# GpSimd makes one of the eight inflow quads of each unit in a fused Mamba and mixture-of-experts kernel

## What is computed

```
deltaA   = exp(einsum('bdl,dn->bdln', delta, A))
deltaB_u = einsum('bdl,bnl,bdl->bdln', delta, B, uc)
state    = deltaA[t] * state + deltaB_u[t]
y[t]     = einsum('bdn,bn->bd', state, C[t])
```

## Time and profile before

| | us |
|---|---|
| median of 3 runs | 899.54 (898.86 to 904.14) |
| the profiled execution, its own time | 906.28 |
| its span in the trace | 904.5 |
| unit 0: from its first inflow to that of unit 1 | 80.8 |
| units 1, 2, 3, 4, 5 | 75.3, 74.3, 74.3, 74.4, 73.2 |
| units 6, 7 | 70.9, 62.6 |
| from there to the end (the last bookkeeping, the experts, the last layer norm) | 250.4 |

### The profile page before, as it was taken

One profiled execution on the slowest core, in us unless ns is written; L12 is line 12 of the kernel. 1 busy time (PEld: TensorE's weight loads), 2 busy tenths in 40 slices (PEclk: granted clock), 3 DMA queues, 4 the chain that ended last, 5 costly groups with the idle time before them and its releaser, 6 DMA issues. The chain is left out here.

```text
span 904.5 us, 11867 instructions
## 1 busy us (share of the span) xinstructions
PE 615.8 (68%) x2649; PEld 294.8 (33%) x2649; DVE 707.4 (78%) x1358; ACT 446.4 (49%) x904; POOL 583.6 (65%) x540
## 2 busy tenths in 40 slices
PE   3855768667685786865877766656540999889820
PEld 2221111222232131221222212212130888888820
DVE  2037888998998998999899899999932577777654
ACT  3545746655637646465464662523310555454425
POOL 5023566586698779779679959968864355554533
PEclk8675586786587576588769655556555899999975
DMA  3047546566467857646746655765102556566546
GB/s 81 0 101 174 134 93 155 136 151 140 104 163 157 229 127 162 150 110 157 166 120 152 141 135 137 162 146 133 38 27 80 161 174 179 163 174 173 170 135 176
DMA packets 67572, 123.64 MB, mean 137 GB/s; under 512 B 10240, under 2 KB 44864, under 8 KB 59312
## 3 DMA queue, kind: packets, MB, share of 16 engines
q1 hardware_dynamic: 63184, 113.90, 52.2%
q0 software_dynamic: 4320, 8.99, 3.2%
HBM read 100.21 MB, written 16.35 MB: 129 GB/s over the span
## 5 line engine op out<-in xcount | busy, mean ns | idle before, releaser
L509 POOL TENSOR_TENSOR hc<-hs,Crep 128x1024 f32<-128x1024 f32 x128 | 306.4, 2394 | 134.3 <-DVE hs L1246 107.8
L1246 DVE TENSOR_TENSOR_SCAN hs<-bank,state,flow 128x512 f32<-128x512 f32 x256 | 314.5, 1268 | 40.4 <-ACT bank L1017 34.4
L1017 ACT ACTIVATE bank<-bank,negA 128x512 f32<-128x512 f32 x256 | 166.8, 660 | 187.1 <-PE bank L724 186.6
L724 PE MATMUL bank<-dparts,sel 96*128 96x512 bf16 x256 | 130.5, 522 | 129.0 <-DVE hs L1246 120.5
L1236 DVE TENSOR_TENSOR flow<-flow,bank 128x2048 f32<-128x2048 f32 x64 | 145.1, 2267 | 13.0 <-issue 12.4
L724 PEld LDWEIGHTS bank<-dparts,sel 96*128 96x128 bf16 x256 | 27.9, 111 | 311.9 <-DVE hs L1246 256.7
L1168 ACT ACTIVATE flow<-bank,b1T 128x128 f32<-128x128 f32 x284 | 80.8, 368 | 81.1 <-PE bank L898 81.1
L733 PE MATMUL bank<-hc,kc 128*32 128x512 f32 x512 | 101.6, 878 | 17.6 <-DVE yg L1254 14.7
L898 PE MATMUL bank<-flow 128*128 128x128 f32 x568 | 83.3, 292 | 13.9 <-issue 6.9
L623 POOL DMA_INDIRECT results<-flow,idn x71 | 69.8, 982 | 33.4 <-issue 33.4
L682 PE MATMUL bank<-hT,wtapT 128*128 128x512 f32 x128 | 76.9, 741 | 15.9 <-ACT hT L953 11.6
(11 more groups left out here) (172 smaller groups left out, 885.1 us busy)
## 6 DMA issues: line engine op xcount, KB each, us to landing
flow<-du_d SPq DMA_DIRECT2D x64, 1024.0 KB, 7.2
flow<-L_ffn_W SPq DMA_DIRECT2D x71, 256.0 KB
dparts<-part SPq DMA_DIRECT2D x96, 64.0 KB, 3.1
xg<-xs SPq DMA_DIRECT2D x71, 66.0 KB
du_d<-du SPq DMA_DIRECT2D x32, 128.0 KB, 2.4
hs<-results SPq DMA_DIRECT2D x16, 256.0 KB, 4.4
xin<-L_attn_x SPq DMA_DIRECT2D x8, 256.0 KB, 3.3
out<-hc SPq DMA_DIRECT2D x8, 256.0 KB, 2.4
```

The lines of the kernel that those rows point to most:

```text
L509: nc.gpsimd.tensor_tensor(hc[:, Q % 2, two, :], hs[:, Q % 2, two, :], Crep[u % 2][:].unsqueeze(1).broadcast_to([P, 2, T]), ALU.mult).then_ ...
L724: nc.tensor.matmul(dbank[G % 3][:], sel[:, g // 4 % 4, :], dparts[u % 2][:, 4 * (g // 16) + g % 4, :])\
L1017: nc.scalar.activation(dbank[G % 3][:], dbank[G % 3][:], ACT.Exp, scale=negA[:, ch:ch + 1]).then_inc(s_ex, 1)
L1246: nc.vector.tensor_tensor_scan(hs[:, Q % 2, j, :], dbank[G % 3][:], flow[Q % 3][:, j, :], state[:, Q // QUADS % 2, Q % QUADS, j:j + 1], AL ...
```

## The change

POOL makes the inflow of quad 6 of each unit, as two products of 128x1024, behind its `times_c` of slots 9 and 10. It reads B from a copy in SBUF, `Bcopy`, which is the same memory as `xnT`. ACT makes the copy at the end of the unit before (`copy_b`). DVE leaves that `inflow` out; its scan at g = 24 waits for both products instead. The seven other inflows stay on DVE and go on reading B from PSUM. The rest are counts and waits that follow from it.

```diff
+        Bcopy = xnT
@@ SP
-                after(sp, s_bu, QUADS * (u - 1))
+                after(sp, s_bu, inflows_before(QUADS * (u - 1)))
+                after(sp, s_bp, 2 * (u - 1))
@@ POOL
+            def inflow_pair(u, pair):
+                Q = QUADS * u + POOL_QUAD
+                two = slice(2 * pair, 2 * pair + 2)
+                if pair == 0:
+                    pool.wait_ge(s_dul[Q % 3], 16 * (Q // 3 + 1))
+                    pool.wait_ge(s_bc, u + 1)
+                nc.gpsimd.tensor_tensor(flow[Q % 3][:, two, :], flow[Q % 3][:, two, :],
+                                        Bcopy[:].unsqueeze(1).broadcast_to([P, 2, T]), ALU.mult).then_inc(s_bp, 1)
@@ POOL host(j), right behind times_c
+                    if slot in (9, 10):
+                        inflow_pair(j, slot - 9)
@@ PE spread_b
-                after(pe, s_bu, QUADS * u)
+                after(pe, s_bu, inflows_before(QUADS * u))
+                after(pe, s_bc, u)
@@ ACT
+            def copy_b(u):
+                act.wait_ge(s_br, u + 1)
+                after(act, s_mf, 4 * (u - 2) + 3)
+                nc.scalar.copy(Bcopy[:], Brep[:]).then_inc(s_bc, 1)
@@ ACT xnT_evac
+                act.wait_ge(s_bp, 2 * min(u + 2, UNITS))
@@ ACT host(j)
+                    if g == 31 and late:
+                        copy_b(j + 1)
@@ DVE inflow
-                    dve.wait_ge(s_br, u + 1)
+                    dve.wait_ge(s_bc, u + 1)
@@ DVE scan
-                    dve.wait_ge(s_bu, Q + 1)
+                    if Q % QUADS == POOL_QUAD:
+                        dve.wait_ge(s_bp, 2 * (Q // QUADS) + 2)
+                    else:
+                        dve.wait_ge(s_bu, inflows_before(Q + 1))
@@ DVE host(j)
-                    if g % 4 == 0:
+                    if g % 4 == 0 and g // 4 != POOL_QUAD:
                         inflow(QUADS * j + g // 4)
```

More of the change, by code:

```diff
@@ L256, in mamba_moe @@
         s_bu = sem("inflow_done")
+        s_bc = sem("B_copied")
+        s_bp = sem("inflow_pairs_done_by_pool")
         s_sc = sem("scan_done")
@@ L309, in mamba_moe, with inflows_before @@
         s_out = [sem(f"out_stored{r}") for r in range(4)]
+        POOL_QUAD = 6
+        def inflows_before(Q):
+            return Q - (Q + QUADS - 1 - POOL_QUAD) // QUADS
         def tile_of(q, j):
@@ L1154, in _ @@
             act.wait_ge(s_negA, 1)
+            copy_b(0)
             for j in range(UNITS):
```

## The result

| | before | after |
|---|---|---|
| median | 899.71 us (4 runs, 898.86 to 904.14) | 921.88 us (4 runs, 921.16 to 922.67) |
| ratio, 95% interval | | 1.0228 (1.0197 to 1.026) |
| the profiled execution, its own time | 906.28 | 921.38 |
| its first scan starts at | 72.17 | 67.43 |

The change makes the kernel 22.2 us slower. The two profiled executions are only 15 us apart, because that of before began its scans 4.7 us late; from the first scan on they can be compared. Of the 22.2 us the scans hold 20.6 by these two traces; the rest is not placed. The table gives each unit from its first scan to the first scan of the next (unit 7 to the end of its last scan), which is 1 to 2 us off the spans by inflows shown ahead.

The account below looks back on a forecast made before the run. DVE was taken to set the scan phase's length, but POOL has no gap where its products go; unit terms 4.2 + 2.3 + 7.8 + 0.6 + 1.0 + 2.1 = 18.0 us on 899.5 gave 917.5 us, range 908.5 to 926.5.

Parts of the forecast that it names:

- The product's price: POOL's new product flow times Bcopy, priced like times_c: 2.31 us until the next instruction starts.
- The scan of g = 24: DVE's scan in unit 4 waits for both POOL products: 3.8 us later, not 2.35 earlier.
- The chain by `cnmr`: First product delays POOL's back_rstd, then ACT's xns, silus and decay, then DVE's scan of g = 25: +2.31 us.
- The unit's end: DVE's comparison L1288 lies blocked through POOL's indirect DMA and last product: unit end +2.6 us in units 2 to 4.
- rival 3: Indirect DMAs do not hold L1288 back at the end of units 2 to 4: 911.2 us, chance 0.2.
- Units 5 and 6: L1288 narrowly gets in behind slot 14's product: +0.6 and +1.0 us, otherwise +3.5 and +4.5.
- rival 1: L1288 is caught at the end of units 5 and 6 as well: 923.9 us, chance 0.24.
- Unit 1: No indirect DMAs, POOL has room at the end, L1288 meets the last product as before: +2.3 us.
- Rival 2: Products done before DVE reaches the scan of g = 24, each unit keeps 2.35 us: 880.7 us, chance 0.03.
- (a): Unit 0: POOL's products lie across delta_u and ahead of rest_delta, delaying mid_part and the scans: +4.2 us.
- (b): Units 1 to 5: POOL's first product stands ahead of cnmr, so the scan of g = 25 is late: +2.31 us.
- (c): Units 2 to 4: the block of one_hots at the unit's end moves with POOL; these units forecast at +2.6 us each.

Follow-up runs that it names:

- the first experiment: The changed kernel with back_rstd ahead of POOL's first product in slot 9 instead of behind it; 919.9 us, ratio 1.0212 (1.0169 to 1.0254).

## Why the prediction came out

The time, 921.88, lies 4.4 us above the forecast and inside its range. The units of the scans hold 2.6 us of that (20.6 against 18.0), most of it in unit 1; the rest is not placed by the two traces. By its own steps:

- **The product's price**: taken as 2.31, it is 2.30 (437.64 - 435.34). Right.
- **The scan of g = 24**: +3.8 forecast; from the unit's first scan it starts 55.72 us on in unit 4, before 51.95, so +3.77. The wait of 6 us is there in units 1 to 6.
- **The chain by `cnmr`**: +2.31 forecast; g = 25 is 58.47 us on after 56.15, +2.32. Right in size. But it was not the only bound there: the first experiment took it away and no gain is shown. Calling the bound by g = 24 and g = 27 "off the chain" did no harm to the sum (g = 27 is +2.41), but it would have misled anyone who repaired the order only.
- **The unit's end**: +0.3 us beyond the chain forecast (2.6 less 2.3), and 0.5 measured in units 2 to 4 (2.82 less 2.32). The size holds, but in part by luck, for the victim was another, which the prediction had not considered. The cast, an instruction ahead of the comparison, came up 0.61 us into the indirect DMA and was held for 2.82; the comparison behind it took 0.23. The mark of the prediction by which L1288 at 0.3 us supports rival 3 would have led astray: it should have been the time of the whole `one_hots`.
- **Units 5 and 6**: the narrow cases, +0.42 and +1.55 against 0.6 and 1.0. `one_hots` slipped in, so rival 1 fell. Timeline of unit 5 of after, DVE:

```profile
531.92 0.45 DVE L1318 CAST topf<-topi 128x8 f32<-128x8 uint32 x1
532.40 0.23 DVE L1321 TENSOR_TENSOR oh<-kc,topf 128x64 f32<-128x64 f32 x1
```

- **Unit 7**: 2.12 against 2.1. **Unit 0**: 3.95 against 4.2; `delta_u` took 2.82 beside the first product as forecast, and leaving that one unit's quad on DVE gave 3.8 back.
- **Unit 1**: 4.07 against 2.3, the one mis-sized term. "copy_b: nothing" looked only at the spot in a steady unit; in unit 0 the copy stands ahead of L992, and TensorE waits 0.92 us for it. Together with the lower granted clock at that place (0.61) it made a scan wait of 1.12. The other 0.65 us of the 1.77 are a smaller wait behind it (0.32) and parts that are not traced.
- **Load of quad 6, `low_delta`, SP's queue**: counted at nothing. DVE's waits for loads before inflows are 13.3 us in all after 13.0, and the new products had no idle time before them in any unit (the page's group of L527: 0.0).
- **Rival 2 and the sign**: the room of 134.3 us that POOL seemed to have the earlier trace rows has become 116.8, so 17.5 of the products' 37.5 us did find it, but not where it would have spared DVE the wait for them. With the room used at the right place, quad 1, the kernel is 1.1% faster instead of 2.3% slower.
- **Rival 3** said that indirect DMAs do not hold L1288 back, so that it is through before the last product. In time it is refuted (units 2 to 4 are 2.8 longer, not 0.5). What in such a DMA blocks is not settled, see below.

Of the three places, (a) is worth 3.8 us by the run with unit 0 on DVE. (b) is worth 13.2 where it is the only bound (the scan of g = 25 is 2.3 later in each of units 2 to 5, the rest lies in unit 1 and at the ends of units), and no gain is shown for it in after, where the bound by g = 24 is as high. (c), the moving of the block, adds 0.5 in each of units 2 to 4 and takes 1.9 and 2.5 away in units 5 and 6, where cast and comparison now take 0.45 + 0.23 and before took 0.17 + 2.47 and 0.14 + 3.01; that is why unit 5 is only 0.42 longer in spite of a chain that is 2.3 longer.

## What to carry to other kernels

Work moved to an engine with free time is worth only what that engine's free time is at the place where the result is wanted; read the timeline there, and everything that the moved instruction is put ahead of. Here two chains of equal height ended at one place, and repairing one of them showed no gain: before an order is repaired, work out what is late next, here to within 0.1 us. A cast of eight columns on VectorE cost 0.14 us here or two whole GpSimd products (4.89), by where it started, so put it where GpSimd has a gap.

## What the runs showed of the hardware beyond what was expected

A cast of eight columns, one input, was held by GpSimd as the comparison with two inputs was (2.45 us in unit 4 of before, 0.23 in unit 5 of both kernels with only `one_hots` moved): 2.82 us in unit 4 of after, 4.89 in the second-quad kernel with `one_hots` moved, where two products followed each other, and 0.14 in unit 4 of before, where nothing held it. In unit 5 of after the cast came up beside a running product and took 0.45 us, until that product had ended. In the long cases it came up ahead of the product (0.43 us in unit 4 of after, 456.35 - 455.92) and was held all the same.

When it was held is not a simple matter of overlap with the product. In after the cast came up 0.61 us into an indirect DMA (455.92 - 455.31) and in the second-quad kernel 0.84 (444.80 - 443.96), and both were held until the product behind had ended. Before, these two were not held, with the DMA and then DVE of unit 6:

```profile
587.79 1.01 POOL L544 DMA_INDIRECT xs<-xn,pos  x1 [0.17 <-issue]
...
588.09 0.14 DVE L1285 CAST topf<-topi 128x8 f32<-128x8 uint32 x1
```

and of unit 4:

```profile
443.66 1.01 POOL L544 DMA_INDIRECT xs<-xn,pos  x1 [0.16 <-issue]
...
444.51 0.14 DVE L1285 CAST topf<-topi 128x8 f32<-128x8 uint32 x1
```

They came 0.30 and 0.85 us into the DMA. With `delta_u`, a two-input instruction, free at 0.47 and the comparison held at 0.48, no one threshold in the DMA fits all six. What was the same in these held cases is that POOL's next product followed the DMA within 0.04 us and ran first. In unit 4 of before it followed as closely, and the cast was through 0.05 us ahead of it. Where no product followed, nothing long was seen: in the kernel after with `one_hots` moved, the cast came up 0.60, 0.57 and 0.57 us into a DMA at the start of units 3 to 5 and took 0.38, 0.14 and 0.14. And in the case of `delta_u` it was POOL that paid. Its product behind the DMA, in unit 2 of before, took 2.83 where it takes 2.36 elsewhere:

```profile
266.18 2.83 POOL L509 TENSOR_TENSOR hc<-hs,Crep 128x1024 f32<-128x1024 f32 x1
```

It also matters what the instruction met first. In the second-quad kernel the casts that came up 0.79 to 0.85 us into a DMA were held through both products behind it (4.88 to 4.93). At the start of unit 2 of the same kernel the cast came up 1.07 us into the first product, took 1.31 and was through as that product ended, not held by the second. `delta_u` in unit 0 of after did the same: it came up 0.61 us into a product and got in ahead of the next, which followed without a gap and took 3.31. Which part of an indirect DMA holds a VectorE instruction, and which engine wins at its end, stays open.
